# The second layer norm's row step on ScalarE, with its transposes as a step of their own

## The reference

```
n   = (x - mean) / sqrt(var + 1e-5)
q   = n @ w_q             # 16 heads of 16
k,v = [ctx; ctx] @ w_kv   # one head of k and v for all
x   = x + softmax(q k^T / 4) v @ w_concat
x1  = x
y   = (x1 - mean) / sqrt(var + 1e-5)          # over the row
core= (y - mean(y)) * rsqrt(var(y) + 1e-12)   # the second norm, of y
ao  = core * attn_nw + attn_nb
top-1 gate: argmax(ao @ wg) of 8 experts, a place in it by cumulative sum, at most 256 rows each
out = x1 + y + coef0 * res_mlp(ao) + coef1 * gate * expert(ao)
```

## Time and profile before

| | us |
|---|---|
| median of three runs | 441.46 |
| lowest, highest | 439.79, 446.71 |
| the profiled execution | 442.74 |
| its span | 440.1 |
| TensorE busy in it | 372.5 |
| VectorE busy | 202.7 |
| ScalarE busy | 190.1 |
| GpSimd busy | 158.2 |

### The profile page before, as it was taken

One profiled execution on the slowest core, in us unless ns is written; L12 is line 12 of the kernel. 1 busy time (PEld: TensorE's weight loads), 2 busy tenths in 40 slices (PEclk: granted clock), 3 DMA queues, 4 the chain that ended last, 5 costly groups with the idle time before them and its releaser, 6 DMA issues. The chain is left out here.

```text
span 440.1 us, 6595 instructions
## 1 busy us (share of the span) xinstructions
PE 372.5 (85%) x2298; PEld 298.4 (68%) x2298; DVE 202.7 (46%) x612; ACT 190.1 (43%) x373; POOL 158.2 (36%) x219
## 2 busy tenths in 40 slices
PE   4758676867998799899899879879999999999992
PEld 2435444655776677677677767768888888888881
DVE  3255778838545965965955957521001110101110
ACT  3213474557246646546546628443143322332210
POOL 4322134238174068168168061265002121212122
PEclk9865658989699999899899999989999999999997
DMA  6567670231023362472402400193213586571212
GB/s 200 182 181 218 216 184 18 74 82 38 15 72 116 98 227 74 113 255 75 106 24 73 108 26 15 42 370 92 56 41 96 167 246 189 136 220 13 24 18 30
DMA packets 51336, 49.84 MB, mean 113 GB/s; under 512 B 4764, under 2 KB 48488, under 8 KB 51304
## 3 DMA queue, kind: packets, MB, share of 16 engines
q1 hardware_dynamic: 48232, 45.21, 33.7%
q0 software_dynamic: 3072, 4.21, 5.2%
HBM read 33.65 MB, written 15.63 MB: 112 GB/s over the span
## 5 line engine op out<-in xcount | busy, mean ns | idle before, releaser
L860 ACT ACTIVATE h<-ubank,vecT 128x256 f32<-128x256 f32 x128 | 53.7, 471 | 129.3 <-PE ubank L591 129.1
L751 PE MATMUL mbank<-w2r,h 128*128 128x256 f32 x256 | 66.1, 399 | 0.5 <-ACT h L860 0.5
L591 PE MATMUL ubank<-ao,w1r 128*128 128x256 f32 x256 | 63.8, 396 | 0.0
L559 POOL DMA_INDIRECT out_rows<-yrow,rowid x16 | 24.8, 1550 | 103.3 <-DVE yrow L1078 73.2
L751 PE MATMUL mbank<-w2e,h 128*128 128x256 f32 x256 | 60.8, 379 | 0.0
L591 PE MATMUL ubank<-ao,w1e 128*128 128x256 f32 x256 | 60.0, 379 | 0.0
L751 PEld LDWEIGHTS mbank<-w2r,h 128*128 128x128 f32 x256 | 49.4, 198 | 7.6 <-issue 0.6
L591 PEld LDWEIGHTS ubank<-ao,w1r 128*128 128x128 f32 x256 | 49.5, 200 | 6.6
L591 PEld LDWEIGHTS ubank<-ao,w1e 128*128 128x128 f32 x256 | 48.5, 190 | 6.6
L751 PEld LDWEIGHTS mbank<-w2e,h 128*128 128x128 f32 x256 | 48.2, 190 | 6.3
L949 DVE TENSOR_TENSOR p_lo<-p,p_hi 128x512 f16<-128x512 f32 x64 | 46.4, 738 | 11.9 <-ACT p L825 11.7
(11 more groups left out here) (127 smaller groups left out, 517.4 us busy)
## 6 DMA issues: line engine op xcount, KB each, us to landing
w1e<-in_L_ffn_inter_w SPq DMA_DIRECT2D x8, 1024.0 KB, 5.8
w2e<-in_L_ffn_output_w SPq DMA_DIRECT2D x8, 1024.0 KB, 8.8
qstack<-dram_q SPq DMA_DIRECT2D x16, 384.0 KB, 4.5
dram_q<-qpart SPq DMA_DIRECT2D x8, 384.0 KB, 2.6
dispatched<-zrow SPq DMA_DIRECT2D x4, 516.0 KB, 5.2
drow<-dispatched SPq DMA_DIRECT2D x8, 258.0 KB, 3.6
xs<-in_x SPq DMA_DIRECT2D x8, 256.0 KB, 3.4
ctxs<-in_ctx SPq DMA_DIRECT2D x8, 256.0 KB, 3.6
```

The costliest lines, as they stand in the source:

```text
L559: pool.indirect_dma_start(out=out[:, :], in_=yrow[:, e % 2, t, :], in_offset=None, compute_op=ALU.add, out_offset=bass.IndirectOffsetOnAxi ...
L591: last = nc.tensor.matmul(dst, w[kc], v[kc], start=(kc == 0), stop=(kc == len(w) - 1))
L751: last = nc.tensor.matmul(b[:, 0:D], h[:, n % 2, f, t * P:(t + 1) * P], w2[:, f, :], start=(f == 0), stop=(f == FC - 1))
L860: nc.scalar.activation(h[:, n % 2, f, :], place["up", n, c][:, j, :], ACT.Gelu_apprx_tanh, bias=vecT[:, col:col + 1]).then_inc(sem("gelu_d ...
```

## The change

The row step `(x1 - mean) * r` on VectorE becomes `x1 * r + (-mean * r)` on ScalarE. VectorE makes `negmean` in `ln2`, GpSimd makes `shift` after the power, ScalarE makes `core`. The transposes on TensorE and the affine on ScalarE get a step `coreT`, 1.00 later in the plan. GpSimd's residual stays at `core`. Between `core` and `coreT` the plan has, for unit 0, `PV(1,3)`, `low(1,4)` and `o(1,1)`; for units 1, 2 and 7 nothing; for units 3 to 6 the next unit's `M` (and a spill's DMA on the sync engine).

```diff
-        "proj": [20.34], "ln2": [22.4], "core": [23.87], "gate": [29.59], "loc": [37.82], "gw": [2.43],
+        "proj": [20.34], "ln2": [22.4], "core": [23.87], "coreT": [24.87], "gate": [29.59], "loc": [37.82], "gw": [2.43],
...
-        "proj": [19.72], "ln2": [21.77], "core": [23.95], "gate": [26.61], "loc": [39.06], "gw": [14.41],
+        "proj": [19.72], "ln2": [21.77], "core": [23.95], "coreT": [24.95], "gate": [26.61], "loc": [39.06], "gw": [14.41],
...
-        "proj": [21.09], "ln2": [21.42], "core": [23.76], "gate": [30.12], "loc": [39.86], "gw": [17.25],
+        "proj": [21.09], "ln2": [21.42], "core": [23.76], "coreT": [24.76], "gate": [30.12], "loc": [39.86], "gw": [17.25],
...
+        negmean = sb("negmean", [P, NBATCH], f32)
+        shift = sb("shift", [P, NBATCH], f32)
...
-            if kind == "core":
+            if kind == "coreT":
                 return [("m", "cT") + k]
...
                 pool.tensor_tensor(yy[:, c, :], va2[:, c, :], mhalf[:, :, :], ALU.pow).then_inc(sem("ln2_pow"), 1)
+                pool.wait_ge(sem("ln2_pow"), u + 1)
+                pool.tensor_tensor(shift[:, c], negmean[:, c], yy[:, c, 1], ALU.mult).then_inc(sem("ln2_shift"), 1)
...
-                     "M": max_rows, "B": scores_T, "PV": weigh, "oT": oT, "proj": proj, "core": cT, "gate": lg,
+                     "M": max_rows, "B": scores_T, "PV": weigh, "oT": oT, "proj": proj, "coreT": cT, "gate": lg,
...
+            def normed(u):
+                act.wait_ge(sem("ln2_shift"), u + 1)
+                if u >= 2:
+                    act.wait_ge(sem(f"disp_in{u % 2}"), 16 * T * (u // 2))
+                for t in range(T):
+                    i = T * u + t
+                    ins = nc.scalar.activation(core[:, u % 2, t, 0:D], xs[:, i, :], ACT.Identity,
+                                               bias=shift[:, i:i + 1], scale=yy[:, i, 1:2])
+                ins.then_inc(sem("core_ready"), 1)
...
-                     "oT": oT, "core": affine, "ein": lambda e: affine(U + e), "gw": gate_exp, "up": up}
+                     "oT": oT, "core": normed, "coreT": affine, "ein": lambda e: affine(U + e), "gw": gate_exp, "up": up}
...
+                own(V.tensor_scalar(negmean[:, c], mv2[:, c, 0], -1.0, None, ALU.mult))
                 own(V.tensor_scalar(va2[:, c, 0], mv2[:, c, 1], 1e-5, None, ALU.add))
...
-            def normed(u):
-                dve.wait_ge(sem("ln2_pow"), u + 1)
-                if u >= 2:
-                    dve.wait_ge(sem(f"disp_in{u % 2}"), 16 * T * (u // 2))
-                for t in range(T):
-                    i = T * u + t
-                    ins = V.tensor_scalar(core[:, u % 2, t, 0:D], xs[:, i, :], mv2[:, i, 0:1], yy[:, i, 1:2],
-                                          ALU.subtract, ALU.mult)
-                ins.then_inc(sem("core_ready"), 1)
```

More of the change, by code:

```diff
@@ L119, in xattn_moe_ffn_kernel @@
         for kind in ("load", "ln1", "xn", "ctxT", "xT", "kv", "q", "qrest", "qmid", "qlast", "vt", "oT", "proj", "ln2",
-                     "core", "gate", "loc"):
+                     "core", "coreT", "gate", "loc"):
             if kind != "load" or u >= 2:
@@ L1081, in _ @@
             calls = {"small": small, "vec": vectors, "ln1": ln1, "xn": norm_x, "qrest": q_rest, "qlast": q_last, "vt": vt, "A": score_max, "M": max_rows, "low": low_part, "o": o,
-                     "proj": proj, "ln2": ln2, "core": normed, "gate": gate, "loc": place_rows, "gw": gate_weight,
+                     "proj": proj, "ln2": ln2, "gate": gate, "loc": place_rows, "gw": gate_weight,
                      "ein": rowids, "down": down}
```

## The result

The changed kernel is slower: ratio 1.016 of the kernel before, 95% interval 1.010 to 1.0221 (medians 448.11 and 443.62 us). Timed again later with more runs it was 1.0132 (1.0057 to 1.0208). A repeated run of the kernel before against itself gave 1.0006 (0.9961 to 1.0051). The ratios leave out runs more than 1.5% above the fastest of their kernel, and since the runs of one kernel scatter by some 3% here (the kernel before from 436.59 to 451.23 us in one series), this can leave few of a series, so I give the medians of all runs beside a ratio where they say something else.

A forecast was written before the change was run, and what follows sets the result against it. TensorE's queue was taken to bound the kernel (busy 372.5 of 440.1 us). The unit terms 0.9 + 0.9 + 1.5 + 0.75 - 0.5 + 0.3 = +3.85 us, on the median 441.46, gave 445.3 us, range 441.5 to 449.5.

The forecast's parts named there:

- unit 0 +0.9: Row step waits behind two exponentials on ScalarE; transposes start about 73.55 in place of 72.26; cost +0.9 us.
- unit 1 +0.9: Row step waits for ScalarE's exponentials; transposes at 97.15 in place of 96.26, TensorE already idle there; cost +0.9 us.
- unit 2 +1.5: Row step waits behind ScalarE's last gelus, losing the two engines' parallelism; transposes and gate products later; cost +1.5 us.
- units 3 to 5 +0.75: Transposes 1.4 us late, mostly hidden by idle before q and the new order of banks; 3 x 0.25 us.
- unit 6 -0.5: ScalarE is free while VectorE is in the maxima; transposes at 261.1 in place of 261.63; gain 0.5 us.
- unit 7 +0.3: Nothing hides the chain from the power to the transposes; negmean, shift and the ScalarE pair cost +0.3 us.
- price of a pair: Two row-step ACTIVATEs in a row on ScalarE: 1.02 to 1.27 us, taken as 1.02.
- rival 1: TensorE's clock falls once or twice more after longer gaps, some 1.6 us a fall: 447 to 449 us; chance 0.17.
- a fall there is possible, not likely: On TensorE's clock at unit 2: its gap grows to 2.2 us, about unit 6's, which kept the clock.
- units 0, 1 and 7 have theirs already: Argument against more clock falls: these three units already have such falls in the kernel before.
- Rival 2: ScalarE's row step holds back neighbouring units' exponentials or gelus in units 0 to 5: over 2% slower, 451 us; chance 0.13.
- Rival 3: Freed VectorE sends row maxima sooner; if exponentials follow, units 0 and 3 to 5 cost nothing: +2.2 at most, 443; chance 0.18.

The follow-up runs named there:

- unsplit run: The changed kernel with `coreT` right behind `core` again in all units, row step still on ScalarE; ratio to the kernel before 1.0305 (1.025 to 1.0361).

## Why the prediction missed, point by point

- **The direction and the mechanism of the lateness** held: slower, by TensorE's waits for ScalarE's `core`, and mostly by ScalarE's queue ahead of the row step and not by its price.
- **The terms**, at equal clock: unit 0 +0.9 forecast, +1.4 measured; unit 1 +0.9 and +0.7; unit 2 +1.5 and +1.1 (the gap grew by 1.48, a part was given back before the next projection); units 3 to 5 +0.75 and +0.1; unit 6 -0.5 and -0.4; unit 7 +0.3 and +0.4. Sum +3.85 and +3.3. That the sums lie so near is partly luck: unit 0's half microsecond too little and the 0.65 too much of units 3 to 5 cancel. It is luck too that the first profiled executions differ by 3.83 us (446.57 against 442.74): the stretch of the table grew by 6.3 us there, and the part ahead of it happened to be 2.6 shorter. The price of a pair was 1.09, between the ends given, not the 1.02 taken.
- **The step that failed**: the sum has no term for the clock, and rival 1, which has one, got 0.17, by the two sentences "a fall there is possible, not likely" and "units 0, 1 and 7 have theirs already". Unit 2 had the fall in all four profiles, 3.4 to 6.8 us of half clock, and unit 0's stretch didn't stay as it was: it went from 3.4 to 6.8 or 10.2 us. On the means of four, unit 0 cost +2.4 us and unit 2 +2.9, where 0.9 and 1.5 were forecast; unit 3's -1.1 and unit 7's +1.4 are the clock's too, in the main. In all the clock is some 1.7 of the 5.0 us between unit 0 and the experts. I had judged unit 2 by unit 6, where 2.12 us of idle kept the clock; in the three later profiles of before the same 2.12 us lost it, and the fourth loses it in unit 2 with 0.66 and 0.43 us of idle. The sum was made from one profiled execution, and that execution was one without those falls.
- **What remains.** The two timings, 5.9 to 7 us by their ratios, are above the 5.0 us of the stretch, but their intervals reach down to 0.57%. The whole profiled executions differ by 3.9 us in the mean of four (442.74, 442.34, 442.10, 445.87 against 446.57, 445.88, 448.04, 448.23), near the 4.5 and 3.9 of the medians of all runs; the part ahead of unit 0 and the experts are 0.4 us shorter each in the changed kernel's profiles. Whether the loss is nearer to 4 or to 7 us stays open; at 7, some 2 us of it have no place in the profiles.
- **Rival 2** (over 2%) didn't come: q(5) was freed by the banks. The unsplit run, with that taken away, is at 3%, so what was said against this rival held.
- **Rival 3** has the size right for units 3 to 5 (+0.1 in place of +0.75) and wrong for unit 0, and its path is not borne out. In unit 3 the copy of the row maxima starts 7.88 us after the projection in place of 8.17, and the exponentials behind it 14.92 in place of 14.76: the maxima go out earlier and the exponentials don't follow.

## What to carry to other kernels

Moving a step to an engine with room costs what stands ahead of it in that engine's queue, more than its duration: one place earlier in the queue in three units was worth some 0.8 to 1% here, and the order of PSUM banks 1.5 to 1.7%. Price a longer gap of TensorE with the clock that may fall behind it, here 1.1 to 1.6 us for each 3.4 us at half clock at most places and nothing at one, and read that risk from several executions of the kernel before, since a single one shows only where the clock happened to fall. Compare two profiles piece by piece at equal clock; then terms of half a microsecond can be read that the total hides.

## What the runs showed of the hardware that was not expected

The clock's falls differ between executions of one and the same program: in the kernel before, 20.4 to 30.6 us at half clock between the first projection and the experts, which is 242.9 to 247.2 us of time. In unit 2 the falls went with where the clock's stretches stood against the program, and, at the same place, with the late row step. In unit 6 2.12 us of idle kept the clock in one profile of before and lost it in three, and in the changed kernel 0.47 us lost it in all four. Small matmuls put into a gap took away the fall behind it in unit 2, in unit 7 (3.70 to 2.22 us from the transposes to the gate) and in unit 1 of the kernel before, not in unit 1 of the changed one, and no filled version is shown to be faster for it. The row step done twice came with 51 us at half clock. What the chip goes by in lowering the clock was not tried and stays open.
